# First sequence of a hybrid S6 / mixture-of-experts / S5 kernel: delta ahead of the S5 matrices, its product waiting for x alone, W3 unscaled with halved router weights, the rotation's temporary rows in a PSUM bank

## What is computed

```python
x = x + s6(layernorm(x))      # delta = softplus(d_raw @ Wdt + bdt); h = exp(delta*A)*h + delta*B*xs; y = C*sum(h)
x = x + moe(layernorm(x))     # 8 experts, the best 2 of each token, softmax over those two
x = x + s5(layernorm(x))      # x_t = Lambda_bar * x_(t-1) + B_bar u_t; y = Re(C x) + D u
x = x + moe(layernorm(x))

logits = xf @ Wg
top_w, top_i = jax.lax.top_k(logits, 2)
top_w = jax.nn.softmax(top_w, axis=-1)
y = einsum(silu(xf @ W1) * (xf @ W2), W3);  out = sum over experts of weight * y
```

## Time and profile before

| | |
|---|---|
| median of three executions | 1850.45 us |
| profiled execution: device time / span of its instructions | 1861.63 us / 1859.7 us |
| busy: PE, PE weight loads, DVE, ACT, POOL | 1351.0, 617.7, 1514.5, 1281.5, 1513.9 us |
| scans L1251, products L947, decays L837 | 1192.1, 1193.6, 681.9 us |
| granted TensorE clock, mean | 0.86 |
| DMA moved | 121.89 MB, mean 66 GB/s |

### The profile page before, as it was taken

How to read it: one execution, slowest core, us unless ns; L and a number is a source line. 1 busy time by engine, 2 the same in 40 slices (tenths; PEclk the granted TensorE clock), 3 DMA queues, 4 the chain that set the end, 5 groups by cost and what they waited for, 6 DMA issues and landing times.

```text
span 1859.7 us, 19053 instructions
## 1 busy us (share of the span) xinstructions
PE 1351.0 (73%) x5928; PEld 617.7 (33%) x5928; DVE 1514.5 (81%) x2105; ACT 1281.5 (69%) x2275; POOL 1513.9 (81%) x888
## 2 busy tenths in 40 slices
PE   4336458777886887778776878778787778668958
PEld 1001123234342343324342343324332343324535
DVE  4879988898889889898899888888888988895222
ACT  4547668687877778777777778777787777755423
POOL 0899999978998799977998899987998799983312
PEclk9557569889987989879897989879898898979979
DMA  3601411122111311132101401132111321100000
GB/s 87 212 34 71 164 46 51 49 91 97 57 40 48 148 51 33 54 104 96 55 25 50 162 29 51 49 106 81 51 51 49 102 85 52 46 29 1 7 1 6
DMA packets 38747, 121.89 MB, mean 66 GB/s; under 512 B 5875, under 2 KB 21110, under 8 KB 26358
## 3 DMA queue, kind: packets, MB, share of 16 engines
q1 hardware_dynamic: 37062, 120.67, 18.3%
q10 hardware_dynamic: 1584, 0.01, 0.0%
HBM read 109.13 MB, written 11.53 MB: 65 GB/s over the span
## 4 chain that ended last, share of the span: by engine, by line
PE 27%; ACT 18%; DVE 15%; POOL 14%; issue 8%; DVEq 0%; POOLq 0%; ACTq 0%
DVE h L1251 10%; POOL w L947 9%; PE bankH L565 8%; ACT da L837 5%; PE bankY L579 5%; PE bankG L565 5%; ACT yk L798 4%; ACT L837 3%; PE ys L633 2%; POOL x L890 2%; PE bankG L512 2%; DVE aq L1189 1%; PE bankY L559 1%; ACT L785 1%; ACT sq L785 1%
## 5 line engine op out<-in xcount | busy, mean ns | idle before, releaser
L1251 DVE TENSOR_TENSOR_SCAN h<-da,w 128x512 f32<-128x512 f32 x1024 | 1192.1, 1206 | 158.3 <-ACT da L837 133.0
L947 POOL TENSOR_TENSOR w<-ur,br 128x1024 f32<-128x1024 f32 x512 | 1193.6, 2365 | 33.1 <-DVE h L1251 21.2
L837 ACT ACTIVATE da<-dr,al 128x511 f32<-128x511 f32 x1024 | 681.9, 687 | 221.9 <-DVE h L1251 212.5
L633 PE MATMUL ys<-h,wsum 128*32 128x512 f32 x2048 | 320.9, 703 | 208.5 <-DVE h L1251 189.2
L565 PE MATMUL bankH<-nT,w 128*128 128x512 f32 x512 | 301.8, 673 | 89.7 <-DVE aq L1189 85.3
L890 POOL TENSOR_TENSOR x<-x,yk 128x512 f32<-128x512 f32 x128 | 163.1, 1274 | 211.2 <-ACT yk L798 210.6
L579 PEld LDWEIGHTS bankY<-w,aq 128*128 128x128 f32 x2048 | 262.8, 203 | 87.0 <-issue 65.0
L579 PE MATMUL bankY<-w,aq 128*128 128x128 f32 x2048 | 270.5, 289 | 12.4 <-DVE aq L1189 7.9
L565 PE MATMUL bankG<-nT,w 128*128 128x512 f32 x432 | 243.8, 648 | 24.6 <-DVE aq L1189 24.6
L798 ACT ACTIVATE yk<-bankY,rt 128x128 f32<-128x128 f32 x512 | 151.8, 364 | 121.5 <-PE bankY L579 107.8
L633 PEld LDWEIGHTS ys<-h,wsum 128*32 128x32 f32 x2048 | 42.9, 115 | 408.5 <-DVE h L1251 373.2
(11 more groups left out here) (187 smaller groups left out, 1135.8 us busy)
## 6 DMA issues: line engine op xcount, KB each, us to landing
br<-b_rows SPq DMA_DIRECT2D x64, 1024.0 KB, 5.0
dr<-d_rows SPq DMA_DIRECT2D x16, 1024.0 KB, 7.1
ur<-u_rows SPq DMA_DIRECT2D x16, 1024.0 KB, 8.4
d_rows<-vh SPq DMA_DIRECT2D x16, 256.0 KB
u_rows<-th SPq DMA_DIRECT2D x16, 256.0 KB
xnew<-in_L_attn_a_x_dram SPq DMA_DIRECT2D x8, 256.0 KB, 5.3
w<-in_L_ffn_W_dram SPq DMA_DIRECT2D x2, 1024.0 KB, 11.1
x<-in_L_attn_a_x_dram SPq DMA_DIRECT2D x8, 256.0 KB, 9.1
```

What stands on the lines that cost most here:

```text
L633: ins = nc.tensor.matmul(ys[32 * q:32 * q + 32, :], wsum[:, :], h[:, (DUOS * t.b + 2 * group + q // 2) % H_RING, q % 2, :], start=(n == 0) ...
L837: A(da[duo % D_RING][:, k % 2, 1:L], dr[:, half, q, 1:L], ACT.Exp, scale=nega[:, QUADS * half + q, n:n + 1]).then_inc(decay_ready, 1)
L947: G.tensor_tensor(w[:, turn_duo % W_RING, :, :], ur[:, half, q:q + 2, :], br[:, chunk % B_RING, row:row + 1, :].to_broadcast([128, 2, L]), ...
L1251: V.tensor_tensor_scan(h[:, turn_duo % H_RING, k % 2, :], da[duo % D_RING][:, k % 2, :], w[:, turn_duo % W_RING, k % 2, :], 0.0, ALU.mult, ...
```

## The change

Delta of the first sequence moves ahead of the S5 matrices on DVE (`SETUP_AT` from slot 80 to 87), and PE turns the matrices after in2 and in3 instead of ahead of them. POOL's product of delta and xs of the first sequence waits for in0 and in1 only. The copies `mb`, `mc` move ahead of the table of rotations; the table's two temporary rows go from SBUF (`rT`, `tq`) to PSUM bank Y, and its one-column steps become `tensor_scalar` with pointer scalars. `scale_outputs` and PE's wait for it go; the routing computes weights that are half as large, with another sequence of steps: one mask difference in place of a difference and a sum before the gap's tanh, and after it a new `tensor_scalar` on the 128x4 tile, then a product and a sum whose operands are R(5), the 128x4 tile and R(2).

```diff
-SETUP_AT = PRE_AT + 10
-MATRICES_AT = PRE_AT + 11
+SETUP_AT = PRE_AT + 17
+MATRICES_AT = PRE_AT + 17
 TURN_AT = PRE_AT + 18
-SCALE_AT = 52
@@ PE, moe
-                        if n == 0:
-                            pe.wait_ge(outputs_scaled, QUADS)
@@ POOL
-            def scale_outputs():
-                for n in range(QUADS):
-                    yield SCALE_AT + 3 * n
-                    ...
-                    G.tensor_scalar(part, part, 0.5, None, ALU.mult).then_inc(outputs_scaled, 1)
             def pre_a(t):
-                        for m in range(4):
+                        for m in range(2 if known(i, 1) else 4):
                             pool.wait_ge(drained[BANK[f"in{m}"]], t.before(f"in{m}") + 1)
-                weave(pair, [gates(t)] + ([scale_outputs()] if known(t.b, 1) else []) + tasks_of(t, pre_a, post, late))
+                weave(pair, [gates(t)] + tasks_of(t, pre_a, post, late))
@@ DVE, diagonal_setup
                 yield TURN_AT
+                v.wait_ge(matrices_turned, 1)
+                link(V.tensor_copy(mb[:, :, :].rearrange("p n c -> p (n c)"), banks["Y"][:, 0:256]))
+                link(V.tensor_copy(mc[:, :, :].rearrange("p n c -> p (n c)"), banks["Y"][:, 256:512]))
+                settle()
                 ...
                 while n < L:
-                    one, two = rT[:, 0:n], tq[:, 0, 0:n]
+                    one, two = banks["Y"][:, 0:n], banks["Y"][:, 256:256 + n]
                     link(V.tensor_scalar(one, sinT[:, 0:n], s_, None, ALU.mult))
                     link(V.tensor_scalar(two, cosT[:, 0:n], s_, None, ALU.mult))
-                    link(V.tensor_tensor(S(19), s_, s_, ALU.mult))
-                    link(V.scalar_tensor_tensor(s_next, s_, 2.0, c_, ALU.mult, ALU.mult))
+                    link(V.tensor_scalar(S(19), s_, s_, None, ALU.mult))
+                    link(V.tensor_scalar(s_next, s_, c_, 2.0, ALU.mult, ALU.mult))
                     settle()
                     link(V.scalar_tensor_tensor(cosT[:, n:2 * n], cosT[:, 0:n], c_, one, ALU.mult, ALU.subtract))
                     link(V.scalar_tensor_tensor(sinT[:, n:2 * n], sinT[:, 0:n], c_, two, ALU.mult, ALU.add))
-                    link(V.scalar_tensor_tensor(c_next, c_, c_, S(19), ALU.mult, ALU.subtract))
+                    link(V.tensor_scalar(c_next, c_, c_, S(19), ALU.mult, ALU.subtract))
                     settle()
                 ...
-                v.wait_ge(matrices_turned, 1)
-                link(V.tensor_copy(mb[:, :, :].rearrange("p n c -> p (n c)"), banks["Y"][:, 0:256]))
-                link(V.tensor_copy(mc[:, :, :].rearrange("p n c -> p (n c)"), banks["Y"][:, 256:512]))
@@ DVE, routing
-                link(V.tensor_tensor(R(4), R(2), R(1), ALU.subtract))
-                link(V.tensor_tensor(R(5), R(2), R(1), ALU.add))
+                link(V.tensor_tensor(R(5), R(1), R(2), ALU.subtract))
                 yield SLOT[f"lg{m}"] + 5
                 v.wait_ge(gap_tanh_ready, 2 * c + m)
-                link(V.tensor_tensor(R(4), R(4), spread(rc[:, 2, :]), ALU.mult))
-                drain(f"lg{m}", V.tensor_tensor(rt[:, 0, :, :], R(4), R(5), ALU.add))
+                link(V.tensor_scalar(rc[:, 2, :], rc[:, 2, :], -0.5, 0.5, ALU.mult, ALU.add))
+                link(V.tensor_tensor(R(5), R(5), spread(rc[:, 2, :]), ALU.mult))
+                drain(f"lg{m}", V.tensor_tensor(rt[:, 0, :, :], R(5), R(2), ALU.add))
```

More of the change, by code:

```diff
@@ L278, in hybrid_kernel @@
         ones_ready = sem("ones_ready"); angles_ready = sem("angles_ready"); rates_ready = sem("rates_ready"); matrices_ready = sem("matrices_ready")
-        setup_done = sem("setup_done"); outputs_scaled = sem("outputs_scaled"); setup_chain = sem("setup_chain"); rows_spread = sem("rows_spread")
+        setup_done = sem("setup_done"); setup_chain = sem("setup_chain"); rows_spread = sem("rows_spread")
         matrices_turned = sem("matrices_turned"); setup_a = sem("setup_a"); diagonal_a = sem("diagonal_a")
@@ L858, in rstd @@
                 G.tensor_tensor(nm[:, k, :], nm[:, k, :], minus[:, :], ALU.mult).then_inc(rstd_ready[k], 1)
-            def scale_outputs():
-                for n in range(QUADS):
-                    yield SCALE_AT + 3 * n
-                    if n == 0:
-                        pool.wait_ge(expert_loads, 16 * EXPERT_LOADS)
-                    part = w3[:, 2 * n:2 * n + 2, :, :].rearrange("p e k c -> p (e k c)")
-                    G.tensor_scalar(part, part, 0.5, None, ALU.mult).then_inc(outputs_scaled, 1)
             def pre_a(t):
```

## The result

The changed kernel takes 1884.18 us (median; 1881.63 to 1885.69), against 1850.42 us: 33.8 us more, a ratio of 1.0185 (95% interval 1.0169 to 1.0202). Slower, as forecast, but the time lies above the range of 1838 to 1872 us.

A forecast was written before the change was run, and what follows sets the result against it. POOL was taken to bound turn 0, and later turns the chain of waits through the routing's last step. Terms -6.5 - 6.1 + 22 + 0.5 = +10 us on the median 1850.45 gave 1860 us, range 1838 to 1872.

The forecast's parts named there:

- the needless link: Before the first scan: POOL's delta product waited behind the SiLU of in3, which has nothing to do with it.
- the 6.5 us in the sum: At the start: POOL's first product comes 6.5 us earlier, at 46.1, with 5 and 8 for ends.
- both parts together: Earlier start of POOL, -6.5 us, and no scaling of W3 in turn 0, -6.1 us: -12.6 in all.
- rT's wait: Last step of the table on DVE: could wait for a POOL product's end, up to 2.3 us, first scan at 53.5.
- The rival of the table: One-column steps of the table wait for POOL too, losing 5.6 us of the start's gain: 1866 us; chance 0.10.
- first rival: In the routing only the two-operand product waits, the small `tensor_scalar` doesn't: 8.7 us, at 85% 7.4, so 1845; chance 0.28.
- The routing's mechanism: After the tanh, the new `tensor_scalar` and the product behind it both wait for POOL's products; 26 us; chance 0.50.
- +22 us for the routing: Routing's term in the sum: 85% of 26 us of waits reaches the end.
- 26 us in the sum: Routing waits: 19.3 us at seven places, 6.4 at six, 0.3 at one, nothing at the last two.
- the `tensor_scalar` gets in at 0.50: Routing at 911.87: the small step enters at POOL's next boundary, the product waits to 2.85; 2.76 us at each of seven places.
- The share that reaches the end, 85%: Routing: 85% of the 26 us of waits (22 us) lengthens the kernel, other engines' gaps swallowing some.
- item 4: PE's clock: a shift of all times may add or take longer turns, 3 us each, either way.

The follow-up runs named there:

- variant with the old routing: The changed kernel with the routing steps of the kernel before, W3 unscaled; 1839.04 us, ratio 0.9941 to the kernel before.
- the order alone: The kernel before with only delta ahead of the matrices and POOL's product waiting for in0 and in1 only; 1852.18 us, ratio 1.0003.
- new routing alone: The kernel before with only the new routing steps, W3 still scaled by one half; 1895.93 us, ratio 1.0255.
- second trace of before: The kernel before, unchanged, traced a second time; median 1850.46 us, ratio 1.0005, span of the traced execution 1853.6 us.
- factor in PSUM: The changed kernel with the small 128x4 routing step writing to the PSUM bank, where the product reads it; 1850.17 us, ratio 0.9998.
- one more step: The changed kernel with the old routing steps and one added PSUM-to-PSUM DVE copy behind the product; 1853.20 us.
- difference in PSUM: The changed kernel with the masks' difference written to the PSUM bank, the small 128x4 step left from SBUF to SBUF; 1872.14 us, ratio 1.0106.
- four single columns: The changed kernel with the small 128x4 routing step split into four one-column steps, the product keeping two SBUF reads; 1882.27 us, ratio 1.0173.
- without the scaling: The kernel before without `scale_outputs` and PE's wait for it; 1843.95 us, ratio 0.9959.

## Why the prediction was wrong, point by point

**The bound and the start held.** POOL bounded turn 0, the SiLU was the needless link, the transfers cost what they had cost; the 6.5 us in the sum for the earlier product were 6 to 7. For both parts together the sum had -12.6; the variant with the old routing measured -11.4. That DVE's table becomes the next in line, first scan at 51 to 52, was about right: 50.50 with fast matmuls at the start, 52.4 to 54.0 in the three traces of the new order where they were as slow as in the trace it was worked out from. So was rT's wait for a product (1.13 us in place of 0.49). That the order alone would be worth nothing was not in the prediction, but follows from its reading of the 1.30 us steps: it was expected so before that run.

**The rival of the table** fell: steps of one column take 0.20 us beside a running product. So the 128x4 step and the one-column step differ, though both go from SBUF to SBUF. The `tensor_scalar` of one column didn't wait, those of 4, 64 and 256 columns did; steps with two tensor reads waited at one column as at 32. A slip in the first rival's sum, 8.7 us where 0.5 at seven places and 0.8 at six make 8.3, changes nothing at its 1845.

**The routing's mechanism held**, as forecast: both steps wait for POOL. Two terms of the price were mis-sized, the second by more. Together the sum had +22 us for the routing, and the runs showed 45.

*The waits, 26 us in the sum, were 35.5.* This is the time from the first of the last steps to the next instruction behind them, over 16 places 42.7 us, less 7.2. The step that failed here is "the `tensor_scalar` gets in at 0.50": I let each waiting step in at the next end of a product. It came so at 695.63; in the next turn, in the same place, it did not (timelines of DVE and POOL):

```profile
695.63 0.49 DVE L1162 TENSOR_SCALAR rc<-rc 128x4 f32<-128x4 f32 x1
696.15 2.28 DVE L1163 TENSOR_TENSOR rt<-rt,rc 128x32 f32<-128x32 f32 x1
...
914.09 5.08 DVE L1162 TENSOR_SCALAR rc<-rc 128x4 f32<-128x4 f32 x1
919.21 0.19 DVE L1163 TENSOR_TENSOR rt<-rt,rc 128x32 f32<-128x32 f32 x1
...
909.86 9.29 POOL L935 TENSOR_TENSOR w<-ur,br 128x1024 f32<-128x1024 f32 x4
```

POOL goes through four products without a gap, and DVE's four columns stand for 5.08 us, past two ends of products. At four of the seven places with products back to back the small step let one or two ends pass (3.53, 4.65, 5.08, 5.12 us). The seven together cost 27.1 us, not 19.3; the six where POOL itself waits for a scan cost 7.7, not 6.4. The one pair of 1.30 us steps in the trace before had each got in at once, and I took two cases for a rule. In the trace of the new routing alone the rule did hold, at all seven places, so whether it holds depends on the execution or on the exact times. The Trainium skill ("SBUF — State Buffer", section "Who interferes with whom") says that in the two-port modes whoever issues first gets the shared pair for the whole instruction. The rows don't contradict that, but a DVE step that had waited for the whole of a product was passed over by the next one, and which of the two wins a boundary no row here explains.

*The share that reaches the end, 85%, was over 100%.* "The gaps of the other engines swallow some" was argued, not read. The new routing alone is the clean case: its waits are 32.9 - 7.2 = 25.7 us, the 26 of the sum, and the time grew by 45.5. Two rows grouped by form of its turn 3, with waits of 3.6 us in all, and the windows of that turn there and in the second trace of before:

```profile
L1174 DVE TENSOR_TENSOR rt<-rt,rc 128x32 f32<-128x32 f32 x2 | 2.5, 1240 | 0.1
L1173 DVE TENSOR_SCALAR rc<-rc 128x4 f32<-128x4 f32 x2 | 1.4, 720 | 0.0
...
642.20:860.60 218.40, 169.29 (x744) 78.53 (x740) 189.52 (x250) 161.69 (x287) 188.33 (x111) 0.88 0.20 68
637.70:849.40 211.70, 160.32 (x740) 73.52 (x740) 186.19 (x249) 161.18 (x287) 188.21 (x110) 0.92 0.21 69
```

Every steady turn there takes 218 us in place of 211.7, 3 us more than its waits, at a lower grant (0.88 against 0.92). That is as much as turns 2 and 5 of the first trace are longer than their neighbours, and in turn 5 the grant was lower too. I had this as item 4, "3 us each, either way", and left it out of the sum as chance. It isn't chance here: it came in every steady turn. Counted from the first scan of turn 1 to the end, against the second trace of before, the traces of the variants have:

| variant | added to the last steps, us | longer, us |
|---|---|---|
| factor in PSUM | 2.9 | 8.5 |
| one more step | 3.7 | 8.2 |
| difference in PSUM | 12.3 | 20.0 |
| four single columns | 23.8 | 33.6 |
| new routing alone | 25.6 | 40.4 |
| the change | 35.4 | 43.3 |

Each delay reached the end whole, and 4 to 15 us came on top. So the step "I count 85% (22 us)" failed, and it weighs more than the first: in the new routing alone the forecast 26 us of waits went with a loss of 45. How much of the extra is PE's clock isn't shown. Between kernels without any delay this stretch differs by up to 11 us (4.5 us shorter without the scaling and with the order alone, 6.6 longer in the first trace), so the single rows are rough. By the medians: start -11.4, from the old routing to the one with the factor in PSUM +11.1, from there to the change +34.0; these three add up to the measured 33.8 because each begins where the last ended, so their sum proves nothing. In the changed kernel the split varies from turn to turn: turn 3 has waits of 3.6 us and is 6.6 us longer than in the second trace of before, turn 4 has 6.5 and is 6.9 longer.

**The median of before** was right, but the trace beside it had two longer turns that none of the four other traces with the routing of before has. Against that trace the change looks 11 us better than it is.

## What to carry to other kernels

Where POOL works from SBUF without pause, a DVE step with two tensor reads, and a `tensor_scalar` of more than one column, want an operand or the output in PSUM, however few elements they have: four columns cost up to 5.1 us. A saving at the start of a long pipeline is paid once, a step on the chain of every turn 14 times; count the second first. And in a chain woven this tightly a delay can cost more than its own length (3.7 us of added steps made some 8 here), so a forecast for it should count the whole delay and lean to the slow side.

## What the runs showed of the hardware that I had not expected

- A DVE step that waits for POOL's SBUF reads can be passed over at the end of a product, once or twice: waits of 3.5 to 5.1 us beside products of 2.3 us. Both kinds did it: the 128x4 `tensor_scalar` in the changed kernel, the 128x32 product in the variant with four single columns. In the traces of the variant with the difference in PSUM and of the new routing alone the small step never was, in 14 waits each, seven of them beside products back to back.
- A `tensor_scalar` of one column from SBUF to SBUF never waited (64 times 142 to 148 ns, 56 of them beside POOL's products), one of four columns did at all 14 places beside those products, and a `tensor_tensor` of one column with two reads waited 2.29 us.
- A delay of 0.24 us on DVE in each routing, 3.8 us in all, cost 12 to 14 us by the medians and some 9 in the traces.
- The four matmuls of the projection of steps and B took 3.75 us in two traces of the kernel before and 1.96 us in that of the changed kernel. The windows view gives a granted clock of 1.00 over that stretch in all three. But the two traces of before hold no record of the grant so early, their first is at 36.41 and 37.30 us; that of the change has its first at 18.24, just ahead of these matmuls. The matmuls of 512 columns ahead of the first record mostly took 1.06 us each (they overlap), as long as later ones at 1.2 GHz, and the first ones behind it 0.59, as at 2.4. So a 1.00 at the start of a view can mean that nothing was recorded.
